# Coordinates of segments 1 to 3: a store and broadcast loads in place of TensorE products

## Chip, core and metric

One core of a Trainium2 chip runs the whole program. The metric is the device time of one execution in microseconds; the time of the kernel before is the median of three runs.

## The reference

Two layers (L0, L1) of deformable attention with an MLP, on `x` of shape 2 x 128 x 32 x 32 in float32. Per layer and batch image:

```
xn  = bn1(x);  q = gconv1x1(xn, qw)                       # 8 groups of 16 channels
off = tanh(pw @ gelu(depthwise6x6_stride4(q) + b)) * 4     # an 8x8 grid of offsets per group
n   = 2 * (grid + off) / 7 - 1                             # normalised x and y of each key
kv  = bilinear_sample(xn, n);  k, v = gconv1x1(kv, kw), gconv1x1(kv, vw)
pos = grid_q - n;  t = sign(pos) * log1p(|pos|)            # 1024 queries x 64 keys, 2 features
bias = w3 . relu(w2 . relu(w1 . t + b1) + b2) + b3         # MLP per query and key, 32 wide
x   = x + out_w @ softmax(q k / 4 + bias) v + out_b
x   = x + w2 @ gelu(w1 @ bn2(x) + b) + b                   # channel MLP 128 -> 512 -> 128
```

Bilinear sampling is written as a product with hat functions: the weight of image pixel (y, x) for a key is max(0, 1 - |cx - x|) * max(0, 1 - |cy - y|), where cx, cy are the key's pixel coordinates.

## The kernel before

The work is a chain of four segments (`SEGS` = 2 layers x 2 images), each with four units (pairs of groups) of 16 steps: 64 steps a segment, 256 in all. One step is a slice of the position-bias MLP for 128 keys: VectorE makes the hidden layer (`first_layer`, L638) into one of three `h1` buffers, TensorE adds corrections (L861) and layer 2 (L887) into two PSUM pairs, ScalarE takes each pair out with a relu (`relu2`, L484), TensorE does layer 3 (L905) of the step before into `scores`.

Every engine has its own instruction stream in an order written out by hand. `BEFORE_SLOTS` gives, for each stage that prepares the next segment, the step of the current segment behind which each engine does it; `AFTER_SLOTS` and `SOFTMAX_SLOTS` do so for attention, MLP and softmax. `plan()` collects them; within a step, softmax stages come ahead of preparing ones. Engines meet through semaphores only. In a step, ScalarE first does the second relu of the step before, then the first relu of this one, then the copy of the scores where one is due, then the planned stages. VectorE does its layer first, then the planned stages. TensorE does corrections and layer 2, then the planned stages, then layer 3.

PSUM has three pairs of banks that go round in a ring (`ring()`): each step takes two, and each planned TensorE stage one more. A pair is used again only when its last user has emptied it.

The preparation of a segment, around the change: `positions` (L670, VectorE) makes pixel coordinates `coord[:, 3]`, one key per partition, 8 columns (4 pairs, x and y). `spread` (L959, TensorE) multiplies each column, broadcast to 128 columns, by the identity, so that every partition gets all 128 x 8 coordinates in a PSUM pair. `features` (L527, ScalarE) makes sign and logarithm of the positions for the bias MLP. `spread_out` (L537, ScalarE) turns the x half into distances `hat_x` and copies the y half to `key_y`, which lies in `work`. `distances` (L544, ScalarE, four parts of two) makes |cy - y| for eight row blocks in `hat_y`. `hats` (L729, VectorE, two parts) turns distances into negated hats; the first part also does `hat_x`. `hat_products` multiplies them: four on GpSimd (L460), four on VectorE (L738). `sample` (L968, TensorE) multiplies them with the transposed image, `sample_out` (L744, VectorE) and `keys_values` (L981, L556) follow. `features_sign` (L686, VectorE) makes the features that SP stores (`store_features`, L378) and loads again spread over partitions (`load_features`, L388).

SP issues all DMAs in program order: per segment the store of features, the loads of the unit, the store of the `fy` parts, then per unit loads, and the two turns of the softmax denominators through DRAM (`invert_sums`).

Of the kernel before, what the change touches and what calls it, by code (L numbers as in the profile page):

```python
# [7 lines left out]
F32 = mybir.dt.float32  # L8
# [57 lines left out]
for _name, _n in [("ident", 128), ("gridq", W), ("gridkv", 2), ("neg_x", 1), ("neg_y", CHUNKS), ("ones", 32), ("own", 2),  # L66
# [11 lines left out]
    ("pool", "conv_products", 1): 31, ("dve", "conv_products", 0): 31, ("dve", "conv_products", 1): 32,  # L78
    ("pe", "image_t", 0): 30, ("act", "image_t_out", 0): 30, ("dve", "conv_sum", 0): 33,
    ("dve", "conv_sum", 1): 34, ("act", "conv_gelu", 0): 33, ("pe", "offset", 0): 35,  # L80
    ("act", "offset_tanh", 0): 35, ("dve", "positions", 0): 38, ("pe", "spread", 0): 37,
    ("act", "features", 0): 37, ("act", "spread_out", 0): 37, ("dve", "features_sign", 0): 40,
    ("act", "distances", 0): 39, ("act", "distances", 1): 40, ("act", "distances", 2): 41,
    ("act", "distances", 3): 42, ("dve", "hats", 0): 43, ("dve", "hats", 1): 45,
    ("pool", "hat_products", 0): 43, ("pool", "hat_products", 1): 45, ("dve", "hat_products", 0): 46,
    ("dve", "hat_products", 1): 47, ("pe", "sample", 0): 48, ("dve", "sample_out", 0): 50,
    ("pe", "keys_values", 0): 51, ("act", "keys_values_out", 0): 51,
}


# [111 lines left out]
PLACE = ring()  # L202


def build(nc, x_in, consts, weights, x_out, features_dram, fy_dram, reciprocals_dram):
    with ExitStack() as ctx:
        def sb(name, shape, dt=F32):
            return ctx.enter_context(nc.sbuf_tensor(name, shape, dt))
# [67 lines left out]
        gelu_ready = sem("gelu_ready")  # L276
        pos_ready = sem("pos_ready")
        logs_ready = sem("logs_ready")
        feat_ready = sem("feat_ready")
        feat_stored = sem("feat_stored")  # L280
        fy_ready = sem("fy_ready")
# [79 lines left out]
        def _(sp):  # L361
            def invert_sums(half):
# [12 lines left out]
                src = bass.AP(tensor=r.tensor, offset=r.offset, ap=[[HALF, G], [0, DH], [1, HALF]])  # L375
                sp.dma_start(den, src).then_inc(reciprocals_spread, 16)

            def store_features(seg):  # L378
                sp.wait_ge(feat_ready, seg + 1)
                sp.dma_start(features_dram[seg].rearrange("c u k q -> k (c u) q"), feat[:]).then_inc(feat_stored, 16)  # L380
# [49 lines left out]
            for unit in range(UNITS):  # L430
                seg, pair = unit // PAIRS, unit % PAIRS
                if pair == 0:
                    store_features(seg)
                    load_features(unit)
                    store_fy(seg)
                else:
                    load_features(unit)
                load_fy(unit)
                if pair < 2 and seg:
                    invert_sums(2 * (seg - 1) + pair)  # L440
# [37 lines left out]
        def _(act):  # L478
# [58 lines left out]
            def spread_out(seg):  # L537
# [3 lines left out]
                emptied("spread", seg, act.activation(hat_x[:], here[:, bank(0)], ACT.Abs, bias=cst("neg_x")))  # L541
                emptied("spread", seg, act.activation(key_y, here[:, bank(1)], ACT.Copy))

            def distances(n):  # L544

                wait_emptied(act, "spread", n // 4)
                for k in (2 * (n % 4), 2 * (n % 4) + 1):
                    act.activation(hat_y[:, k], key_y, ACT.Abs, bias=cst("neg_y")[:, k:k + 1]).then_inc(distances_ready, 1)

# [39 lines left out]
            def gelu_last(part):  # L589
                for c in range(MLP_PARTS):  # L590
# [3 lines left out]

            stages = {"q_out": q_out, "gelu_last": gelu_last, "image_t_out": image_t_out, "conv_gelu": conv_gelu,
                      "offset_tanh": offset_tanh, "features": features, "spread_out": spread_out,
                      "distances": distances, "attend_out": attend_out,
                      "keys_values_out": keys_values_out, "exp": exp, "widen_max": widen_max,
                      "mlp_gelu": mlp_gelu}
# [20 lines left out]
        def _(dve):  # L620
# [48 lines left out]

            def positions(seg):  # L670
                wait_emptied(dve, "offset", seg)
                if seg >= 1:
                    wait_filled(dve, "spread", seg - 1)
                    dve.wait_ge(logs_ready, 2 * seg)
                for xy in range(2):
                    ordered(dve.tensor_scalar(coord[:, 0, PAIRS * xy:PAIRS * (xy + 1)], tanh[:, xy], OFF_SCALE,
                                              cst("gridkv")[:, xy:xy + 1], ALU.mult, ALU.add))
                ordered(dve.tensor_scalar(coord[:, 1], coord[:, 0], 2.0, 1.0 / (HD - 1), ALU.mult, ALU.mult))
                ordered(dve.tensor_scalar(coord[:, 2], coord[:, 1], -1.0, None, ALU.add))
                ordered(dve.tensor_scalar(coord[:, 1], coord[:, 2], 1.0, W / 2.0, ALU.add, ALU.mult))  # L680
                ordered(dve.tensor_scalar(coord[:, 3], coord[:, 1], -0.5, None, ALU.add))
                dve.tensor_tensor(pos[:], cst("gridq").unsqueeze(1).broadcast_to([128, 2 * PAIRS, W]),
                                  coord[:, 2].unsqueeze(2).broadcast_to([128, 2 * PAIRS, W]), ALU.subtract)\
                    .then_inc(pos_ready, 1)
# [44 lines left out]
            def hats(n):  # L729

                dve.wait_ge(distances_ready, CHUNKS // 2 * (n + 1))
                if n % 2 == 0:
                    dve.tensor_scalar(hat_x[:], hat_x[:], 1.0, 1.0, ALU.min, ALU.subtract).then_inc(hat_x_ready, 1)
                    dve.wait_ge(hat_x_ready, n // 2 + 1)
                y = hat_y[:, 4 * (n % 2):4 * (n % 2) + 4]
                dve.tensor_scalar(y, y, 1.0, 1.0, ALU.min, ALU.subtract).then_inc(hats_ready, 1)  # L736
# [443 lines left out]
```

## Time and profile before

| | |
|---|---|
| median of 3 runs | 901.35 us (900.37 to 902.82) |
| profiled execution | 902.57 us, its span 900.7 us |
| TensorE busy | 812.3 us (90%) |
| VectorE busy | 714.7 us (79%) |
| ScalarE busy | 676.0 us (75%) |
| GpSimd busy | 69.1 us (8%) |
| products of `spread` (L964) | 64 instructions, 9.8 us busy |
| `spread_out` (L541, L542) | 4 each, 2.7 and 2.4 us busy |
| mean TensorE clock granted | 0.979 of full |

Busy shares are means over the whole span; a stage has its own limit, which the timelines show. In the rows, PE is TensorE, DVE VectorE, ACT ScalarE, POOL GpSimd, SP the queue that issues DMAs.

### The profile page before, as it was taken

Reading aid. Unit: us, or ns where it says so; the run is one execution under the profiler, and the core shown is the slowest. Engines: PE = TensorE matmul, PEld = TensorE weight load, DVE = VectorE, ACT = ScalarE, POOL = GpSimd, SP = SyncE. Lnnn points to the kernel's source line nnn. Section 1 sums busy time; section 2 is a strip of 40 time slices with the busy share of each in tenths; the row PEclk is TensorE's granted clock in tenths of the full one; section 3 lists DMA queues with packets and bytes.
Section 4 is the critical chain, followed back from the end, with each engine's and each line's share of the span. In section 5 each row is a group of like instructions: output and inputs, shape, how many; then the busy total and the mean of one; then the engine's idle time right before and its main releaser. Section 6 shows DMA issues by size and latency. Waiting matters only on the chain.

```text
span 900.7 us, 27769 instructions
## 1 busy us (share of the span) xinstructions
PE 812.3 (90%) x12470; PEld 232.4 (26%) x12470; DVE 714.7 (79%) x498; ACT 676.0 (75%) x775; POOL 69.1 (8%) x40
## 2 busy tenths in 40 slices
PE   2299998899999999788999999988999999999997
PEld 1122222222222222222222222222222222222224
DVE  4699798898876688989885868889888668989843
ACT  1368777978786687896877777797777677888863
POOL 2120013210000004030000000302000000000000
PEclk8589999999999999999999999999999999999999
DMA  4310101020020101002020100102002010100000
GB/s 150 80 30 25 28 9 45 7 53 4 14 54 14 50 3 50 9 3 55 3 64 15 49 4 3 50 8 53 4 4 64 14 50 2 50 27 2 2 15 24
DMA packets 23510, 26.77 MB, mean 30 GB/s; under 512 B 15328, under 2 KB 17504, under 8 KB 23392
## 3 DMA queue, kind: packets, MB, share of 16 engines
q1 hardware_dynamic: 23392, 24.99, 10.4%
q8 instruction: 99, 1.62, 0.8%
q14 instruction: 19, 0.16, 0.1%
HBM read 22.79 MB, written 2.08 MB: 28 GB/s over the span
## 4 chain that ended last, share of the span: by engine, by line
PE 42%; issue 39%; ACT 9%; DVE 5%; POOL 5%; DMA 1%; SPq 0%; ACTq 0%; POOLq 0%
PE pair L887 14%; PE scores L905 13%; ACT h L484 5%; PE pair L861 4%; DVE h L638 3%; POOL conv_prod L356 3%; PE pair L1040 2%; POOL big L464 2%; PE scores L916 2%; PE pair L995 1%; PE pair L1013 1%; PE pair L1031 1%; PE scores L1001 1%; ACT big L586 1%; PE pair L940 1%
## 5 line engine op out<-in xcount | busy, mean ns | idle before, releaser
L638 DVE TENSOR_TENSOR h<-hx,hy 128x2048 f32<-128x2048 f32 x256 | 582.1, 2302 | 76.5 <-PE pair L887 72.4
L484 ACT ACTIVATE h<-pair 128x1024 f32<-128x1024 f32 x512 | 517.6, 1024 | 146.9 <-PE pair L861 104.7
L887 PE MATMUL pair<-h,wts 32*32 32x512 f32 x8192 | 300.6, 605 | 20.5 <-DVE h L638 6.1
L905 PE MATMUL scores<-h,wts 128*32 128x512 f32 x2048 | 275.7, 607 | 0.1
L861 PE MATMUL pair<-fy,u_rows 32*128 32x512 bf16 x1024 | 102.6, 387 | 17.1 <-DMA fy<-fy_dram 17.1
L887 PEld LDWEIGHTS pair<-h,wts 32*32 32x32 f32 x8192 | 66.0, 103 | 82.2 <-ACT h L484 34.7
L861 PEld LDWEIGHTS pair<-fy,u_rows 32*128 32x128 bf16 x1024 | 26.4, 91 | 234.4 <-issue 234.4
L905 PEld LDWEIGHTS scores<-h,wts 128*32 128x32 f32 x2048 | 42.2, 108 | 158.0 <-issue 149.2
L356 POOL TENSOR_TENSOR conv_prod<-qpad,wts 128x288 f32<-128x288 f32 x16 | 34.0, 2153 | 417.7 <-ACT qpad L511 417.7
L464 POOL TENSOR_TENSOR big<-big,hat_x 128x512 f32<-128x512 f32 x16 | 32.4, 2054 | 126.6 <-DVE big L736 126.6
L995 PE MATMUL pair<-const,probs 128*128 128x128 f32 x128 | 20.6, 284 | 21.6 <-ACT h L484 20.8
L494 ACT ACTIVATE probs<-scores,wts 128x512 f32<-128x512 f32 x32 | 22.0, 688 | 23.7 <-PE scores L905 23.5
L765 DVE TENSOR_REDUCE neg_max<-pair 128x8 f32<-128x512 f32 x32 | 22.1, 690 | 20.9 <-PE pair L995 20.9
L916 PE MATMUL scores<-qpad,keys_t 128*32 128x512 f32 x256 | 33.3, 592 | 0.0
L1031 PE MATMUL pair<-work,wts 128*128 128x512 f32 x56 | 27.3, 613 | 0.5
L1040 PE MATMUL pair<-big,wts 128*128 128x512 f32 x56 | 25.9, 605 | 1.1 <-ACT big L586 1.0
L995 PEld LDWEIGHTS pair<-const,probs 128*128 128x128 f32 x128 | 13.7, 143 | 49.8 <-issue 48.1
L794 DVE SCALAR_TENSOR_TENSOR x<-pair,wts,x 128x512 f32<-128x512 f32 x7 | 5.3, 752 | 25.9 <-PE pair L1040 25.9
L578 ACT ACTIVATE probs<-scores,wts 128x512 f32<-128x512 f32 x32 | 21.9, 685 | 3.0 <-PE scores L1001 2.8
L586 ACT ACTIVATE big<-pair,wts 128x512 f32<-128x512 f32 x28 | 17.7, 684 | 8.5 <-PE pair L1031 8.4
L1001 PEld LDWEIGHTS scores<-ident_r,neg_max_wide 128*128 128x128 f32 x128 | 17.2, 190 | 24.4 <-ACT neg_max_wide L572 16.5
L1001 PE MATMUL scores<-ident_r,neg_max_wide 128*128 128x128 f32 x128 | 22.9, 302 | 0.6 <-ACT neg_max_wide L572 0.6
(101 smaller groups left out, 375.0 us busy)
## 6 DMA issues: line engine op xcount, KB each, us to landing
hx<-features_dram SPq DMA_DIRECT2D x64, 128.0 KB, 2.7
hy<-features_dram SPq DMA_DIRECT2D x64, 128.0 KB, 3.1
wts<-weights_dram SPq DMA_DIRECT2D x2, 960.0 KB, 8.4
att_den<-reciprocals_dram SPq DMA_DIRECT2D x7, 256.0 KB
x<-x_dram SPq DMA_DIRECT2D x2, 512.0 KB, 5.7
fy<-fy_dram SPq DMA_DIRECT2D x64, 6.0 KB
fy<-fy_dram SPq DMA_DIRECT2D x64, 4.0 KB
fy<-fy_dram SPq DMA_DIRECT2D x64, 2.0 KB
```

What stands on the lines that cost most here:

```text
L356: return engine.tensor_tensor(out, window, taps, ALU.mult)
L464: pool.tensor_tensor(bilinear[:, k], hat_y[:, k], hat_x[:], ALU.mult).then_inc(bilinear_ready[0], 1)
L484: emptied("z", 2 * g + j, act.activation(h2[j][g % H2_BUFS][:].rearrange("p r n -> p (r n)"), pair_of("z", 2 * g + j)[:], ACT.Relu))
L638: dve.tensor_tensor(h1[g % H1_BUFS][:].rearrange("p c (y x) -> p c y x", x=W), hx[unit % 2][:, :, t].unsqueeze(2).broadcast_to([128, CT, H ...
L861: return pe.matmul(z_of(g, r), u_rows[unit // PAIRS // B][key_rows(r)], y.unsqueeze(2).broadcast_to([32, H // 2, W]), **flags)
L887: ins = pe.matmul(z_of(g, r)[32 * c:32 * (c + 1)], w(l, "w2")[key_rows(r), key_rows(r)], h1[g % H1_BUFS][key_rows(r), c], start=r >= 2, st ...
L905: ins = pe.matmul(scores[phase % 2][32 * r:32 * (r + 1)], w(l, "w3")[:, 32 * t:32 * (t + 1)], h2[rows[0] // 2][step % H2_BUFS][:, r % 2], ...
L916: ins = pe.matmul(scores[phase % 2][k], keys_t[seg % 2][:, u, k], qpad[seg % 2][:, 1 + H // 2 * h:1 + H // 2 * (h + 1), 1:W + 1], start=Fa ...
L995: ins = pe.transpose(pair_of("scores_t", phase)[:, s], probs[:, unit % PAIRS, bank(h)][:, s], cst("ident"))
L1001: ins = pe.matmul(scores[phase % 2][:, 128 * k:128 * (k + 1)], neg_max_wide[:, 2 * k:2 * (k + 1)].rearrange("p n j -> p (n j)"), ident_r[: ...
L1031: ins = pe.matmul(pair_of("mlp_up", n)[:, bank(k)], w(half // 2 // B, "mlp_w1")[:, 128 * c:128 * (c + 1)], xn2[:, bank(half % 2)], start=T ...
L1040: ins = pe.matmul(pair_of("mlp_down", half)[:, 0:HALF], w(half // 2 // B, "mlp_w2")[:, 128 * c:128 * (c + 1)], mlp_h[:, c, bank(half % 2)] ...
```

## The change

For segments 1 to 3, the products of `spread` and the two copies of `spread_out` go. SP stores `coord[:, 3]` to DRAM, 4 bytes at a time (`store_coords`), and, behind the store of the features, loads it twice with a partition step of 0 into all 128 partitions: the x half into `hat_x`, the y half into `key_y` (`load_coords`). ScalarE then makes the distances in x in place (`hat_x_distance`, step 40). The first segment, prepared before the loop, keeps the products. The stages behind the coordinates move later: `distances` by two steps (39-42 to 41-44), `hats` and `hat_products` by two, `sample`, `sample_out` and `keys_values` by three.

```diff
-    ("act", "offset_tanh", 0): 35, ("dve", "positions", 0): 38, ("pe", "spread", 0): 37,
-    ("act", "features", 0): 37, ("act", "spread_out", 0): 37, ("dve", "features_sign", 0): 40,
-    ("act", "distances", 0): 39, ("act", "distances", 1): 40, ("act", "distances", 2): 41,
-    ("act", "distances", 3): 42, ("dve", "hats", 0): 43, ("dve", "hats", 1): 45,
-    ("pool", "hat_products", 0): 43, ("pool", "hat_products", 1): 45, ("dve", "hat_products", 0): 46,
-    ("dve", "hat_products", 1): 47, ("pe", "sample", 0): 48, ("dve", "sample_out", 0): 50,
-    ("pe", "keys_values", 0): 51, ("act", "keys_values_out", 0): 51,
+    ("act", "offset_tanh", 0): 35, ("dve", "positions", 0): 38, ("act", "features", 0): 37,
+    ("dve", "features_sign", 0): 40, ("act", "hat_x_distance", 0): 40, ("act", "distances", 0): 41,
+    ("act", "distances", 1): 42, ("act", "distances", 2): 43, ("act", "distances", 3): 44, ("dve", "hats", 0): 45,
+    ("dve", "hats", 1): 47, ("pool", "hat_products", 0): 45, ("pool", "hat_products", 1): 47,
+    ("dve", "hat_products", 0): 48, ("dve", "hat_products", 1): 49, ("pe", "sample", 0): 51, ("dve", "sample_out", 0): 53,
+    ("pe", "keys_values", 0): 54, ("act", "keys_values_out", 0): 54,
...
+            def store_coords(seg):
+
+                sp.wait_ge(pos_ready, seg + 1)
+                sp.dma_start(coords_dram[seg].rearrange("n k -> k n"), coord[:, 3], allow_slow_non_contiguous=True)\
+                    .then_inc(coords_stored, 16)
+
+            def load_coords(seg):
+                for k in range(2):
+                    sp.wait_ge(bilinear_ready[k], 4 * seg)
+                sp.wait_ge(coords_stored, 16 * seg)
+                for dst, n in ((hat_x[:], 0), (key_y, PAIRS)):
+                    c = coords_dram[seg, n]
+                    sp.dma_start(dst, bass.AP(tensor=c.tensor, offset=c.offset, ap=[[0, 128], [1, 128 * PAIRS]]))\
+                        .then_inc(coords_loaded, 16)
...
                 if pair == 0:
+                    if seg:
+                        store_coords(seg)
                     store_features(seg)
+                    if seg:
+                        load_coords(seg)
                     load_features(unit)
...
+            def hat_x_distance(seg):
+
+                act.wait_ge(coords_loaded, 32 * seg)
+                act.activation(hat_x[:], hat_x[:], ACT.Abs, bias=cst("neg_x")).then_inc(hat_x_distanced, 1)
+
             def distances(n):
 
-                wait_emptied(act, "spread", n // 4)
+                if n // 4:
+                    act.wait_ge(coords_loaded, 32 * (n // 4))
+                else:
+                    wait_emptied(act, "spread", 0)
...
             def positions(seg):
                 wait_emptied(dve, "offset", seg)
+                if seg == 1:
+                    wait_filled(dve, "spread", 0)
+                if seg >= 2:
+                    dve.wait_ge(coords_stored, 16 * (seg - 1))
                 if seg >= 1:
-                    wait_filled(dve, "spread", seg - 1)
                     dve.wait_ge(logs_ready, 2 * seg)
...
                 if n % 2 == 0:
+                    if n:
+                        dve.wait_ge(hat_x_distanced, n // 2)
                     dve.tensor_scalar(hat_x[:], hat_x[:], 1.0, 1.0, ALU.min, ALU.subtract).then_inc(hat_x_ready, 1)
```

## Rows read from the trace of the kernel before

**Rows 1.** Windows, steps 28 to 51: length, busy us (instructions) by engine, clock, DMA, GB/s.
```profile
127.20:206.20 79.00, 69.36 (x1160) 20.81 (x1156) 71.05 (x56) 65.15 (x76) 18.02 (x8) 1.00 0.13 33
...
772.90:835.90 63.00, 61.83 (x1064) 15.46 (x1060) 56.00 (x30) 51.19 (x55) 0.00 (x0) 1.00 0.09 28
```

**Rows 2.** Timeline of PE, steps 37 to 40: start, duration, instruction [idle before <-releaser].
```profile
157.88 1.17 PE L887 MATMUL pair<-h,wts 32*32 32x512 f32 x32
160.16 2.02 PE L964 MATMUL pair<-const,coord 128*128 128x128 f32 x16 [1.11 <-ACT h L484]
...
164.52 1.15 PE L887 MATMUL pair<-h,wts 32*32 32x512 f32 x32 [1.02 <-ACT work L542]
...
166.93 1.17 PE L887 MATMUL pair<-h,wts 32*32 32x512 f32 x32
...
170.21 1.17 PE L887 MATMUL pair<-h,wts 32*32 32x512 f32 x32
```

**Rows 3.** Timeline of ACT, steps 37 to 45.
```profile
163.31 0.67 ACT L541 ACTIVATE hat_x<-pair,const 128x512 f32<-128x512 f32 x1
163.88 0.59 ACT L542 ACTIVATE work<-pair 128x512 f32<-128x512 f32 x1
...
169.05 1.32 ACT L548 ACTIVATE big<-work,const 128x512 f32<-128x512 f32 x2
...
184.87 1.28 ACT L578 ACT_TABLE_LOAD   x1
186.16 0.69 ACT L578 ACTIVATE probs<-scores,wts 128x512 f32<-128x512 f32 x1
```

**Rows 4.** Timeline of PE, steps 42 to 52.
```profile
178.33 0.63 PE L995 MATMUL pair<-const,probs 128*128 128x128 f32 x4 [1.65 <-ACT h L484]
...
189.04 1.15 PE L887 MATMUL pair<-h,wts 32*32 32x512 f32 x32 [0.83 <-DVE h L638]
...
196.98 1.95 PE L976 MATMUL pair<-big,image_t 128*32 128x128 f32 x64
...
202.77 1.17 PE L887 MATMUL pair<-h,wts 32*32 32x512 f32 x32
...
206.21 1.17 PE L887 MATMUL pair<-h,wts 32*32 32x512 f32 x32
...
210.32 1.15 PE L887 MATMUL pair<-h,wts 32*32 32x512 f32 x32 [0.84 <-ACT values L564]
```

**Rows 5.** Timeline of DVE, steps 40 to 47.
```profile
163.44 0.43 DVE L690 TENSOR_TENSOR pos_sign<-pos_sign,pos_abs 128x256 f32<-128x256 f32 x1 [0.97 <-ACT pos_abs L535]
...
174.23 1.23 DVE L736 TENSOR_SCALAR big<-big 128x2048 f32<-128x2048 f32 x1
...
179.00 0.69 DVE L765 TENSOR_REDUCE neg_max<-pair 128x8 f32<-128x512 f32 x1 [1.34 <-PE pair L995]
...
182.19 3.37 DVE L638 TENSOR_TENSOR h<-hx,hy 128x2048 f32<-128x2048 f32 x1
...
186.62 2.28 DVE L638 TENSOR_TENSOR h<-hx,hy 128x2048 f32<-128x2048 f32 x1
188.82 1.28 DVE L742 TENSOR_TENSOR big<-big,hat_x 128x512 f32<-128x512 f32 x2
```

**Rows 6.** DMA view, 163 to 170 us: queue, share of 16 engines; issue, us to landing.
```profile
q1 hardware_dynamic: 1040, 0.13, 11.6%
...
features_dram<-pos_sign SPq DMA_DIRECT2D x1, 128.0 KB, 2.3
```

**Rows 7.** Source view of L399, loads of the features into partitions.
```profile
DMA to landing us min/median/max: 2.2/2.9/3.8
```

**Rows 8.** Timeline of POOL, first convolution products and first hat products inside the loop.
```profile
131.97 10.15 POOL L356 TENSOR_TENSOR conv_prod<-qpad,wts 128x288 f32<-128x288 f32 x4 [80.72 <-ACT qpad L511]
175.53 7.87 POOL L464 TENSOR_TENSOR big<-big,hat_x 128x512 f32<-128x512 f32 x4 [33.42 <-DVE big L736]
```

**Rows 9.** Source view of L759, the second hidden term: duration ns min/median/max.
```profile
L759 DVE TENSOR_SCALAR hy<-hy,wts x16: 745/748/1770, 35.2 to 814.2; 128x1024 f32<-128x1024 f32 x16
```

More of the change, by code:

```diff
@@ L202, with build @@
 PLACE = ring()
-def build(nc, x_in, consts, weights, x_out, features_dram, fy_dram, reciprocals_dram):
+def build(nc, x_in, consts, weights, x_out, coords_dram, features_dram, fy_dram, reciprocals_dram):
     with ExitStack() as ctx:
@@ L278, in build @@
         logs_ready = sem("logs_ready")
+        coords_stored = sem("coords_stored")
+        coords_loaded = sem("coords_loaded")
+        hat_x_distanced = sem("hat_x_distanced")
         feat_ready = sem("feat_ready")
@@ L596, in _ @@
                       "offset_tanh": offset_tanh, "features": features, "spread_out": spread_out,
+                      "hat_x_distance": hat_x_distance,
                       "distances": distances, "attend_out": attend_out,
@@ L1173 @@
     out = nc.dram_tensor("out_dram", (B, C, HW), F32, kind="ExternalOutput").ap()
+    coords = nc.dram_tensor("coords_dram", (SEGS, 2 * PAIRS, 2 * NKV), F32, kind="Internal").ap()
     features = nc.dram_tensor("features_dram", (SEGS, 2, PAIRS, 2 * NKV, W), F32, kind="Internal").ap()
@@ L1176 @@
     reciprocals = nc.dram_tensor("reciprocals_dram", (2 * SEGS, G, HALF), F32, kind="Internal").ap()
-    build(nc, *args, out, features, fy_parts, reciprocals)
+    build(nc, *args, out, coords, features, fy_parts, reciprocals)
     r = run_bass_kernel_spmd(nc, [arrays], core_ids=[0])
```

## The prediction

> **What bounds the kernel now.** I number the steps inside a segment from 0 to 63; step k is TensorE's (PE's) k-th pass through layer 2 (L887), and the numbers below are those of the first segment, which prepares the second; the other two repeat it within a microsecond. I first compared equal stretches of steps (28 to 51) with the view of windows [rows 1]: with preparation 79.0, 78.7 and 79.5 us, in the last segment, which prepares nothing, 63.0. Only these 16 us, three times, are touched by the change. In them VectorE (DVE) is busy for 71.05 of 79.00, PE for 69.36 and ScalarE (ACT) for 65.15, so no engine alone is the limit and the timelines must say whose turn it is.
>
> The timeline of PE around the products [rows 2]: a free step takes 164.52 to 166.93 = 2.42 us, a step with queries and keys 166.93 to 170.21 = 3.28. Step 37 takes 157.88 to 164.52 = 6.64: PE waits 1.11 for a PSUM pair, spends 2.02 on the products, and waits 1.02 more at the end, put down to ACT's L542, since step 38 needs the pair that the spread coordinates occupied. ACT's timeline [rows 3] shows why: ahead of the relu that frees the next pair it does the features, ending with the logarithm, for which DVE waits until 163.44 [rows 5], then L541 and L542 (0.67 and 0.59). From there ACT is nearly gapless to 189.6. Steps 42 and 46 show the hand-over [rows 4]: the transposes at 178.33 wait 1.65 for ACT, but step 46 at 189.04 waits 0.83 for DVE. DVE's timeline [rows 5] has its last long pause before 179.00 (1.34) and then runs without one to beyond step 48. So: ACT first, DVE from about step 45.
>
> **The change part by part.** For the coordinates: out go 16 PE instructions (2.02), a ring entry, L541 and L542 (1.26 on ACT); in come one ACT pass over 128x512 in SBUF (0.71, one of the pair at 169.05 [rows 3]), a store and two loads on SP.
>
> The transfers. Coordinates are ready at about 158.1, the features at 163.87 [rows 5], where SP stores them as before, and only then issues the two loads. The trace has no store of 4-byte pieces. The nearest row is the feature store: 1024 pieces of 128 B, 1040 packets taking 11.6% of 16 engines over 7 us = 12.5 ns each, landed after 2.3 us [rows 6]. I take 2.3; a piece would have to cost about ten times as much (64 per engine, over 100 ns) to land later than 166, which is where it starts to matter. Both ends stay in: nothing, or a late arrival (rival D). The loads, issued at some 164.4 and 165.0, land after 2.2 to 3.8 us going by other broadcast loads [rows 7], so by 168.8. SP has nothing else until step 48 lets it load the next unit, so nothing queues behind them. The Trainium skill, "DMA: Bandwidth & Descriptors", "Rules for kernel authors", says that a strided last dimension lowers to one descriptor per element; that speaks against the store and is the 1024 pieces counted here, but no run shows their price.
>
> The walk without the products. Features still end at 163.4. The two relus behind them run 163.3 to 165.25, so step 39 starts at 165.27 in place of 166.93, step 40 at 168.55 (170.21). ACT reaches the new pass at 170.7, two us after the loads; I cost that wait at nothing. Step 41 starts at 170.97. Then copy of scores (0.69) and the first pair of distances (1.32) stand ahead of the relu that frees the pair for the transposes: they start at 176.15, not 178.33, and DVE's maximum at 176.85, not 179.00 [rows 4, 5]. Lead so far: 2.15.
>
> But ACT has got later work. The distances, at steps 39 to 42 before, now stand at 41 to 44, the last pair behind the table load and exponential of step 44 (1.28 and 0.69 [rows 3]). Step 45 starts at 183.9, the exponential ends at 185.85, the distances at 187.1, two relus at 188.95: step 46 starts at 189.0 against 189.04. ACT's lead is gone; afterwards ACT has room.
>
> DVE now holds the first hats at step 45, the second at 47, its products at 48 and 49, and GpSimd's (POOL's) four products start only behind the first hats, at 183, not at 175.5. Here the price is a wait that both engines show. In the trace before, POOL's four products run 175.53 to 183.40 [rows 8], two of them under DVE's work: the layer of step 45 takes 3.37 in place of 2.28 [rows 5], the second hidden term 1.77 in place of 0.75 [rows 9]. So one product costs DVE 1.09 when DVE has no pause, and the pause before 179.00 has hidden the other two. After the change that pause lies ahead of the hats (174.5 to 176.85), so none is hidden: 4 x 1.09 = 4.36. The Trainium skill, "SBUF — State Buffer", "SBUF: two separate sides", calls the pair of ports of these engines an exclusive lock for the whole instruction. The rows of step 45 agree; the page does not say who gets it next when both wait, which rival C turns on.
>
> DVE from 176.85, start to start: maximum 0.60; hidden terms 1.40; layer of step 45 2.20 (186.62 to 188.82 [rows 5]); hats 1.60 (1.23 less the overlap, and an estimated 0.46 for a quarter of the columns); layers 46 and 47 4.40; hats 1.14; layer 48 2.20; products 1.20; layer 49 2.20; products 1.20; layers 50 to 52 6.60; maximum of step 52 0.69. Sum 25.43, with 4.36 for POOL 29.79: it ends at 206.64. Step 51 of PE needs that maximum, since the pair of the transposes comes next in the ring. It starts at 206.65 against 206.21 [rows 4]: 0.45 late. PE alone, from 189.0 with 2.42 + 3.28 + 2.42 + 2.42 + 3.44 (a step with transposes, 202.77 to 206.21 [rows 4]), would be there at 202.98.
>
> At step 51 the kernel before has its sampling behind it (at 196.98, 1.95 busy [rows 4]; about 1.75 net) and pays for keys and values, 206.21 to 210.32 less 2.42 = 1.69. Now sampling is still to come, 1.75; keys and values at step 54, without the widening of the maximum beside them on ACT, cost about 1.1, so 0.6 less. Per segment 0.45 + 1.75 - 0.6 = 1.6 us lost; three segments 4.8. From step 55 on PE alone sets the pace in both, so nothing is given back.
>
> The profiled execution took 902.57 (span 900.7 and 1.87 around it), which is 1.22 above the median of 901.35. 902.57 + 4.8 = 907.4, as a median **906.2**.
>
> **The rivals.** A is the forecast. B, the faster side: POOL's products cost DVE nothing, because they slip between its instructions. Then DVE's 202.28 is no bound, step 51 starts at 202.98, 3.23 early, less 1.75 plus 0.6: 2.1 gained per segment, 6.2 in all, median 895.1. For it: ACT and PE do lose 4.2 us of step 37, and step 42 is 2.15 earlier on any account. Against it: the rows of 3.37 and 1.77. It decides when less than 1.6 of the 4.36 is really paid.
> E: the lock costs what it did before, two products (2.2 saved against A). Then 0.6 is gained per segment: median 899.5, within what can be told from no change.
> C: POOL gets no turn while DVE is busy. POOL's first convolution products have waited so: four took 10.15 us at 131.97 [rows 8], against 7.87 for four hat products, which did get their turns. Step 51 is then early (203.0), but sampling waits until DVE pauses at 204.6 and POOL has done 4.5 us of products: 209.1, 5.0 late. 1.4 more per segment than A, median 910.4.
> D: the store of small pieces, or the loads, come after ACT at 170.7; every us beyond goes into ACT's chain and on to the transposes. A store of 12 us (against 2.3) brings the loads in at some 174.5, 4 us more per segment than A: 918.
>
> **How the numbers follow.** A 0.45, E 0.20, B 0.17, C 0.12, D 0.06. My walk can be off by 0.7 us per segment, so A's own range is 904 to 908.5. The 8 in 10 range goes from 896.5, nearly B, to 911, beyond C. What a measurement can tell from no change is 0.3%, 2.7 us. Slower: most of A, C and D, 0.57. Within: E, the near edge of A and of B, 0.22. Faster: B and a rest of E, 0.21.
>
> **What would show it.** Right, if step 38 starts less than 4 us behind step 37, step 39 leads by about 1.7, step 46 has no lead, layers and products of DVE at steps 47 and 48 show 1.1 us more, and PE waits for DVE at steps 49 to 51 (some 4 us in a segment). B shows DVE's rows at 2.28 and 0.68; C a POOL product of over 8 us and PE waiting at the sampling; D ACT idle ahead of the new pass on a DMA. I am wrong in the main step if DVE is not what PE waits for at step 51.

## The result and the profile after

The changed kernel takes 917.57 us (median of 4 runs, 913.54 to 919.09) against 901.59 in the runs beside it: ratio 1.0166, 95% interval 1.0145 to 1.0188. That is 16 us slower; the forecast was 5 us slower (906.2), its range ended at 911. Direction right, size wrong by a factor of three. The profiled execution took 919.09, its span 917.3, and the mean clock granted to TensorE fell from 0.979 to 0.963.

Windows over the same steps 28 to 51 of the three segments, columns as in [rows 1] (the last three are clock, DMA share, GB/s), and then two short ones around step 39 of the first segment:

```profile
126.40:211.60 85.20, 73.47 (x1084) 18.08 (x1080) 72.38 (x55) 65.62 (x76) 22.18 (x8) 0.92 0.14 36
348.50:433.00 84.50, 73.69 (x1089) 18.30 (x1086) 72.66 (x55) 66.10 (x77) 22.01 (x8) 0.92 0.16 37
570.00:652.20 82.20, 71.22 (x1084) 17.83 (x1080) 72.42 (x55) 66.00 (x77) 22.00 (x8) 0.94 0.16 38
...
163.00:166.40 3.40, 1.94 (x32) 0.50 (x29) 2.85 (x6) 2.21 (x3) 0.00 (x0) 1.00 0.16 25
166.40:170.00 3.60, 2.84 (x12) 0.50 (x15) 1.31 (x2) 1.94 (x2) 0.00 (x0) 0.52 0.39 78
```

The two short ones in the kernel before:

```profile
163.00:166.40 3.40, 2.38 (x48) 0.51 (x44) 1.99 (x6) 3.07 (x5) 0.00 (x0) 1.00 0.24 39
166.40:170.00 3.60, 3.60 (x60) 0.88 (x56) 3.48 (x2) 3.24 (x5) 0.00 (x0) 1.00 0.00 0
```

Against 79.0 us at a clock of 1.00 in the first stretch before, the stretches take 82 to 85 at 0.92 to 0.94: the full-speed clock (2.4 GHz) was not granted all the time. In the first short window PE has work for only 1.94 of 3.40 us (2.38 before), and behind that the granted clock is 0.52 (1.00 before), nearly the lower level of 1.2 GHz.

PE's timeline of the changed kernel, steps 38 to 51 (L922 is layer 2, L887 before; compare [rows 2, 4]):

```profile
160.95 1.15 PE L922 MATMUL pair<-h,wts 32*32 32x512 f32 x32 [0.53 <-ACT h L505]
...
164.35 0.39 PE L896 MATMUL pair<-fy,u_rows 32*128 32x512 bf16 x2 [0.92 <-issue]
165.26 1.12 PE L922 MATMUL pair<-h,wts 32*32 32x512 f32 x24 [0.52 <-issue]
167.16 2.30 PE L922 MATMUL pair<-h,wts 32*32 32x512 f32 x8 [0.78 <-issue]
169.40 1.94 PE L940 MATMUL scores<-h,wts 128*32 128x512 f32 x8
...
173.48 1.17 PE L922 MATMUL pair<-h,wts 32*32 32x512 f32 x32
...
211.57 1.15 PE L922 MATMUL pair<-h,wts 32*32 32x512 f32 x32 [1.85 <-DVE neg_max L800]
```

Step 39 takes 165.26 to 173.48 = 8.22 us; before it took 3.28. Layer 2 breaks off after 24 of 32 instructions with a gap that the trace puts to nothing ("issue"), and then everything runs at half speed: the eight products of L940 need 1.94 in place of 1.07. In the second and third segment step 39 takes 6.85 and 4.95. At step 51 PE waits 1.85 for DVE's maximum, as forecast.

The transfers, in SP's timeline of the changed kernel (start, time to issue, DMA):

```profile
157.37 0.39 SPq L383 DMA_DIRECT2D coords_dram<-coord  x1
163.87 0.38 SPq L397 DMA_DIRECT2D features_dram<-pos_sign  x1
167.66 0.34 SPq L392 DMA_DIRECT2D hat_x<-coords_dram  x1
```

The loads go when the store of the coordinates has landed, the wait that the waits of SP's queue name ahead of them: some 10.3 us after its issue. In the other segments the store and the loads stand at 379.81 and 390.13, and at 601.27 and 610.22: 10.3 and 9.0.

Steps 28 to 56, from the starts of layer 2, in us (before; after; difference): 94.20, 101.68, 7.48; 93.94, 100.47, 6.53; 94.75, 98.32, 3.57. Together 17.6, less 1.0 gained outside these steps (0.9 of it ahead of the first step 28): 16.6 in the span. They split so. Step 39 at half clock, 4.91 (its length with a fast store, below) less 3.28 = 1.63, three times: 4.9. What step 39 (and 40) takes beyond 4.91: 3.31, 2.26, 0.04 = 5.6. Steps 34 and 35, at half clock for a while: 0.87, 0.96, 0.20 = 2.0. The rest is 5.1; the forecast walk, which is all that I had, says 4.8. Half clock is granted at step 46 of each segment too (0.57 to 0.59), but it costs nothing: steps 45 to 52 take 26.9 us with it here and without it in the first segment of e4 below.

### The profile page after: what moved, and what is told of

It reads as the page before. It is cut to its first block, busy times and chain, and to the rows that moved or that the text cites. A ratio compares the mean times of both kernels' runs of the same rounds, so it can differ in the third digit from the quotient of the medians.

```text
span 917.3 us, 27682 instructions
## 1 busy us (share of the span) xinstructions
PE 825.4 (90%) x12422; PEld 229.1 (25%) x12422; DVE 720.9 (79%) x498; ACT 674.6 (74%) x772; POOL 81.7 (9%) x40
## 4 chain that ended last, share of the span: by engine, by line
PE 56%; issue 18%; ACT 12%; DVE 10%; POOL 2%; DMA 0%; SPq 0%; ACTq 0%; POOLq 0%
PE pair L922 19%; PE scores L940 17%; ACT h L505 8%; DVE h L668 6%; PE pair L896 5%; PE pair L1075 3%; PE scores L951 3%; PE pair L1030 2%; PE pair L1048 2%; PE pair L1066 2%; POOL conv_prod L358 2%; PE scores L1036 1%; DVE big L771 1%; DVE big L777 1%; ACT big L615 1%
## 5 line engine op out<-in xcount | busy, mean ns | idle before, releaser
L505 ACT ACTIVATE h<-pair 128x1024 f32<-128x1024 f32 x512 | 517.0, 1024 | 165.4 <-PE pair L896 115.7
L922 PE MATMUL pair<-h,wts 32*32 32x512 f32 x8192 | 307.9, 613 | 22.4 <-ACT h L505 7.3
L940 PE MATMUL scores<-h,wts 128*32 128x512 f32 x2048 | 281.4, 619 | 0.1
L896 PE MATMUL pair<-fy,u_rows 32*128 32x512 bf16 x1024 | 105.9, 391 | 24.6 <-DMA fy<-fy_dram 16.8
L922 PEld LDWEIGHTS pair<-h,wts 32*32 32x32 f32 x8192 | 66.8, 104 | 86.7 <-ACT h L505 38.8
L940 PEld LDWEIGHTS scores<-h,wts 128*32 128x32 f32 x2048 | 42.3, 109 | 163.4 <-issue 154.7
L485 POOL TENSOR_TENSOR big<-big,hat_x 128x512 f32<-128x512 f32 x16 | 44.9, 2837 | 160.7 <-DVE big L771 160.7
L951 PE MATMUL scores<-qpad,keys_t 128*32 128x512 f32 x256 | 36.0, 636 | 0.0
L1036 PEld LDWEIGHTS scores<-ident_r,neg_max_wide 128*128 128x128 f32 x128 | 17.2, 190 | 24.4 <-ACT neg_max_wide L601 16.5
```

The lines of the kernel that those rows point to most:

```text
L485: pool.tensor_tensor(bilinear[:, k], hat_y[:, k], hat_x[:], ALU.mult).then_inc(bilinear_ready[0], 1)
L505: emptied("z", 2 * g + j, act.activation(h2[j][g % H2_BUFS][:].rearrange("p r n -> p (r n)"), pair_of("z", 2 * g + j)[:], ACT.Relu))
L896: return pe.matmul(z_of(g, r), u_rows[unit // PAIRS // B][key_rows(r)], y.unsqueeze(2).broadcast_to([32, H // 2, W]), **flags)
L922: ins = pe.matmul(z_of(g, r)[32 * c:32 * (c + 1)], w(l, "w2")[key_rows(r), key_rows(r)], h1[g % H1_BUFS][key_rows(r), c], start=r >= 2, st ...
L940: ins = pe.matmul(scores[phase % 2][32 * r:32 * (r + 1)], w(l, "w3")[:, 32 * t:32 * (t + 1)], h2[rows[0] // 2][step % H2_BUFS][:, r % 2], ...
L951: ins = pe.matmul(scores[phase % 2][k], keys_t[seg % 2][:, u, k], qpad[seg % 2][:, 1 + H // 2 * h:1 + H // 2 * (h + 1), 1:W + 1], start=Fa ...
```

## The experiments

Theory after the result: two things were missing from the walk. (1) Without the products PE has too little to do in steps 37 to 39, and its clock falls. (2) The store of 1024 pieces of 4 bytes takes 10 us to complete and holds things up while it is open. Rivals: the later steps alone cost all; falls of the clock come anyway; any store would do the same. Ratios are to the kernel before, run beside each (901.6 us), with 95% intervals.

**e1_warm**: the clock alone. In step 37 eight products of constants, which nothing reads, stand in for the removed ones.

```diff
+            def warm(seg):
...
+                for n in range(2 * PAIRS):
+                    ins = pe.matmul(pair_of("warm", seg)[:, 128 * n:128 * (n + 1)], cst("ident"), cst("ident"), start=True, stop=True)
...
```

> The changed kernel, with eight identity products of 128 columns put back on TensorE at step 37; nothing reads them, and the coordinates still come by DMA. Clock theory (the products had filled TensorE's wait for ScalarE in steps 37 and 38; without them it idles, its clock is granted at half behind step 39, and step 39 takes 8.2, 6.9 and 5.0 us in place of 3.3): the half clock behind step 39 goes, step 39 is back at 3.3 to 4.3, some 8 to 10 us in all, 907 to 910. Store theory (the store of 4-byte pieces, some 10 us till it has landed, holds up instruction fetches and loads, and the clock falls because of that): step 39 stays long, 914 to 918. Slots theory (all of the loss comes from the later slots and the lock of VectorE and GpSimd): no change, 917.

Measured: 918.12, 1.0173 (1.0154 to 1.0191), no gain. The half clock behind step 38 was gone in all three segments, but step 39 still took 4.33, 3.28 and 5.50, and step 38 of the second 3.27, with stalls at full clock as in this row of PE's timeline (1.17 is the usual length):

```profile
165.51 2.22 PE L922 MATMUL pair<-h,wts 32*32 32x512 f32 x32
```

The loads came at 168.99, and ACT's new pass waited 1.12 for them; half clock came elsewhere, at steps 35, 42 and 51 (4.68, 5.94 and 5.77 us long). The filler does what it should at step 39, but the total is no better: the store theory had 914 to 918, the slots theory 917.

**e2_short_spread**: the clock in the kernel before. Of its 8 products of 128 columns only one is left in segments 1 to 3, so seven of the eight columns of coordinates are left out; slots, waits and ACT's copies stay.

```diff
-                for n in range(2 * PAIRS):
+                for n in range(1 if seg else 2 * PAIRS):
```

> The kernel before, with one of the eight products in segments 1 to 3 and the other seven left out; ring, ScalarE's copies and slots as before, no DMA for coordinates. Clock theory: TensorE idles 1.8 us more in step 37, its clock falls behind it in two or three segments, 2 to 3.4 us each: 905 to 911, though work has been taken out. Store theory and slots theory: nothing in this kernel can cost; step 38 waits for ScalarE's copies in any case, 900 to 902.

Measured: 905.5, 1.0037 (1.0027 to 1.0048): work taken away from PE made the kernel slower. PE's timeline, and windows around it:

```profile
159.54 0.46 PE L964 MATMUL pair<-const,coord 128*128 128x128 f32 x2 [1.11 <-ACT h L484]
...
163.91 1.64 PE L887 MATMUL pair<-h,wts 32*32 32x512 f32 x32 [2.59 <-ACT work L542]
165.48 1.94 PE L905 MATMUL scores<-h,wts 128*32 128x512 f32 x8
...
167.90 1.17 PE L887 MATMUL pair<-h,wts 32*32 32x512 f32 x32
```
```profile
157.00:164.00 7.00, 3.30 (x64) 0.94 (x70) 5.90 (x7) 6.93 (x11) 0.00 (x0) 1.00 0.01 2
164.00:168.00 4.00, 4.00 (x59) 0.57 (x71) 2.69 (x3) 1.80 (x2) 0.00 (x0) 0.57 0.20 33
```

The 1.56 us of products that went became wait for ACT's L542 (2.59 in place of 1.02 [rows 2]); then the clock is 0.57, and step 38 takes 3.99 in place of 2.41. The same happens in the third segment (steps 38 and 39); in the second a fall came at step 34, and none behind step 38. So with PE idle there the clock falls in two segments of three, without any of the rest of the change.

**e3_no_store**: the changed kernel without its store, the loads reading rows of the input; only the waits for the store go with it.

```diff
...
-                    c = coords_dram[seg, n]
+                    c = x_in[0, n]
...
```

> The changed kernel without the store of the coordinates: the two loads read rows of the input x instead, at the same place in the queue's order, so the sampling has other coordinates. Clock theory: the half clock behind step 39 stays, step 39 takes 5 to 6.7 in all three segments; only the waits for instructions in the first segment go (1 to 1.5 us): 913 to 917. Store theory: step 39 is back at 3.3, 906 to 908.

Measured: 911.89, 1.0106 (1.0082 to 1.013), between the two theories. Step 39 takes 4.83, 4.94 and 4.91: the stalls are gone, the half clock stays. The store is worth 5.7 us between the medians.

**e4_slots_only**: the kernel before with only the later steps.

```diff
-    ("act", "distances", 0): 39, ... ("dve", "hats", 0): 43, ... ("pe", "sample", 0): 48, ...
+    ("act", "distances", 0): 41, ... ("dve", "hats", 0): 45, ... ("pe", "sample", 0): 51, ...
```

> The kernel before with nothing but the later slots (distances 41 to 44, hats 45 and 47, products 48 and 49, sampling 51, keys and values 54). Clock theory and my walk for the lock: no half clock behind step 39, as the products are there; step 51 starts some 2 us later than before, 1.2 more from sampling, keys and values; 3.2 per segment, 910 to 912. Slots theory: the whole loss, 915 to 918. Store theory: 901 to 903.

Measured: 912.64, 1.011 (1.0091 to 1.013). Steps 28 to 56 take 99.77, 97.27 and 97.26. In the second that is 3.33 more than before; the first has 2.2 on top from half clock in steps 35 and 36, ahead of anything that the edit moves. Steps 45 to 52 take 26.9 in all three segments here, and 26.9 in all three of the changed kernel, although PE has half clock within them in five of these six segments and full clock in one (the first here): PE does not set the pace there.

**e5_warm_no_store**: e3 and e1 together, that is e1's products in step 37, no store, and loads from the input.

> The changed kernel with both: the eight idle products back at step 37, and no store of the coordinates (the loads read rows of x, so the sampling has other coordinates). Three-part theory (later slots with the lock, about 1.6 to 3 us a segment; the store, which holds up instructions and then the loads; half clock behind step 38): the last two are gone, what is left is my walk, 905 to 909, with step 39 at 3.3 and step 40 leading the kernel before by 1 to 1.7. Rival (the falls of the clock do not follow the idling at step 38 but come somewhere in each segment in any case): 911 to 914 as without the store alone.

Measured: 911.27, 1.011 (1.0092 to 1.0128); 905 to 909 was expected. Step 39 takes 3.28 in all three segments, but half clock came at steps 34 to 36 and 51, and the total is the rival's (911 to 914). Without those falls a segment loses some 2.2: the 1.6 of the walk and about 0.5 that the filler itself costs (steps 37 and 38 take 7.91 in place of 7.41). Against e3 the filler gained 0.6 in all.

**e6_slots_no_pool**: e4 with GpSimd's hat products cut to one column in segments 1 to 3, for the price of the lock (in the rows, the wait of VectorE and GpSimd for each other); the other columns are left out.

```diff
-                    pool.tensor_tensor(bilinear[:, k], hat_y[:, k], hat_x[:], ALU.mult).then_inc(bilinear_ready[0], 1)
+                    (pool.tensor_tensor(bilinear[:, k, 0:(1 if seg else 512)], hat_y[:, k, 0:(1 if seg else 512)], hat_x[:, 0:(1 if seg else 512)], ALU.mult)).then_inc(bilinear_ready[0], 1)
```

> The kernel before with only the later slots, and GpSimd's four hat products a segment cut from 512 columns to 1 in segments 1 to 3 (the other columns are left out). Lock theory: VectorE's layers and products of steps 46 to 50 lose their 1.1 us each, step 51 comes 3 to 4 us sooner in each segment: 901 to 905 in place of 912.6. Rival (the late sampling, keys and values and ScalarE's order are what costs): 911 to 913.

Measured: 906.34, 1.0056 (1.003 to 1.0081), with a wide spread (900.59 to 911.04): a little above the 901 to 905 expected, and far from the rival's 911 to 913. The profiled execution took 902.83. DVE's timeline from the maximum of step 44 to the layer behind that of step 52, first e6, then e4:

```profile
177.36 0.69 DVE L765 TENSOR_REDUCE neg_max<-pair 128x8 f32<-128x512 f32 x1 [2.21 <-PE pair L995]
...
187.61 1.23 DVE L736 TENSOR_SCALAR big<-big 128x2048 f32<-128x2048 f32 x1
...
202.82 2.28 DVE L638 TENSOR_TENSOR h<-hx,hy 128x2048 f32<-128x2048 f32 x1
```
```profile
180.27 0.69 DVE L765 TENSOR_REDUCE neg_max<-pair 128x8 f32<-128x512 f32 x1 [2.21 <-PE pair L995]
...
191.55 2.29 DVE L736 TENSOR_SCALAR big<-big 128x2048 f32<-128x2048 f32 x1
...
209.95 2.27 DVE L638 TENSOR_TENSOR h<-hx,hy 128x2048 f32<-128x2048 f32 x1
```

25.46 us without the products of POOL, 29.68 with them: 4.22, where the walk had 4.36.

**e7_contig_store, e8_contig_early**: another form of the store, 128 pieces of 32 bytes (a key's 8 coordinates), one load of all 512 KB into `work` ahead of the features' store, ACT reading with a step of 8 elements; e7 with the later steps, e8 with those of before.

```diff
+        spread_coord = work[:].rearrange("p (k n) -> p n k", n=2 * PAIRS)
...
-                sp.dma_start(coords_dram[seg].rearrange("n k -> k n"), coord[:, 3], allow_slow_non_contiguous=True)\
-                    .then_inc(coords_stored, 16)
+                sp.dma_start(coords_dram[seg], coord[:, 3]).then_inc(coords_stored, 16)
...
```

> The changed kernel with the store in the order of the tile, 32 bytes a partition in one piece (128 pieces in place of 1024), one load of all 4 KB into every partition ahead of the store of the features, and ScalarE reading the coordinates with a step of 8. Store part of the theory: the store lands in some 2 us, no engine waits for instructions, like the kernel without a store: 910 to 913. If it is not the pieces of 4 bytes that are slow: 916 to 919. A read with a step of 8 may cost ScalarE something; nothing expected.

> The same store and load, with the slots of the kernel before (distances 39 to 42, hats 43 and 45, products 46 and 47, sampling 48, keys and values 51) and the distances in x at step 38. Three-part theory: the slots part goes too, ScalarE saves 0.5 us and step 42 leads by 1.2, but the half clock behind step 38 stays (some 2 us where it falls): 899 to 905. Slots-only rival: 898 or less.

Measured: e7 921.34, 1.0215 (1.0195 to 1.0235); e8 910.51, 1.0094 (1.0079 to 1.0109); both lie above all that was expected. The store is fast (issued at 157.08 in e7, the load behind it at 158.50) and step 39 is at 4.9, yet e7 is the slowest of all. The reason is a cost that I had not thought of. ACT's timeline of e8:

```profile
162.92 1.24 ACT L567 ACTIVATE hat_x<-work,const 128x512 f32<-128x512 f32 x1
...
166.07 2.36 ACT L580 ACTIVATE big<-work,const 128x512 f32<-128x512 f32 x2
```

Read with a step of 8, a pass takes 1.24 in place of 0.71 and a pair 2.36 in place of 1.32 (changed kernel, below): 0.53 and four times 1.04, 4.7 us of ACT in each segment. At step 42 PE waits for ACT (2.65 us in the first segment of e7), and half clock follows there in all six segments of the two kernels. So these two do not tell what the store costs.

**e9_transposed**: the fast store without that. VectorE turns the coordinates in blocks of 32x32 and SP stores 32 pieces of 128 bytes; the rest is the changed kernel.

```diff
-                sp.dma_start(coords_dram[seg].rearrange("n k -> k n"), coord[:, 3], allow_slow_non_contiguous=True)\
-                    .then_inc(coords_stored, 16)
+                for b in range(4):
+                    rows = slice(32 * b, 32 * b + 2 * PAIRS)
+                    sp.dma_start(coords_dram[seg, :, 32 * b:32 * b + 32], coord_t[rows]).then_inc(coords_stored, 16)
...
+                    ordered(dve.tensor_scalar(coord_wide[:, 0:2 * PAIRS], coord[:, 1], -0.5, None, ALU.add))
+                    ordered(dve.transpose(coord_t[:], coord_wide[:]))
...
```

> The changed kernel with another layout of the same store and nothing else of it moved: VectorE transposes the coordinates in blocks of 32x32, so that each coordinate's 32 keys lie side by side, and the store is 32 pieces of 128 bytes in place of 1024 of 4; the loads stay two and contiguous, behind the features' store. Theory (the 10 us that the 1024 pieces take to complete cost 5.7 us: instruction fetches of 3.3 to 3.5 us and late loads): the store lands in about 2 to 3 us, no fetch over 1.8 us, step 39 takes 4.9 us in all three segments (the clock's part stays), 911 to 913 us, as without the store. Rival (any store beside the fetches does it, whatever its pieces): step 39 at 5 to 8 us and 916 to 918.

Measured: 912.62, 1.0122 (1.0109 to 1.0135), as the theory said. SP's and PE's timeline:

```profile
157.80 1.28 SPq L387 DMA_DIRECT2D coords_dram<-coord_t  x4
164.07 0.39 SPq L400 DMA_DIRECT2D features_dram<-pos_sign  x1
164.57 0.50 SPq L395 DMA_DIRECT2D hat_x<-coords_dram  x1
```
```profile
165.46 1.36 PE L930 MATMUL pair<-h,wts 32*32 32x512 f32 x32 [0.52 <-ACT h L508]
166.75 1.94 PE L948 MATMUL scores<-h,wts 128*32 128x512 f32 x8
...
170.37 1.17 PE L930 MATMUL pair<-h,wts 32*32 32x512 f32 x32
```

The loads follow the features' store at once. Layer 2 of step 39 is whole, and step 39 takes 4.91 in all three segments, still at half clock (1.94 for L948). The form of the store is worth 5.0 us between the medians.

**e10_transposed_early**: that store, loads ahead of the features' store, and the steps of before (new pass in step 38).

```diff
+    ("dve", "features_sign", 0): 40, ("act", "hat_x_distance", 0): 38,
+    ("act", "distances", 0): 39, ("act", "distances", 1): 40, ("act", "distances", 2): 41,
...
                         store_coords(seg)
+                        load_coords(seg)
                     store_features(seg)
-                    if seg:
-                        load_coords(seg)
...
```

> The store as in e9_transposed, the loads issued ahead of the features' store, and preparation in the steps of the kernel before (distances in steps 39 to 42, sampling in step 48). Theory (later steps cost 1.6 us a segment by the shared lock, the clock 1.6): step 39 at 4.9, the stretch of steps 45 to 51 back to 20 to 21 us, 28 to 56 at 94 to 96 us a segment, 902 to 907 us in all. Rival (the loads land too late for distances in step 39, and ACT loses there what the lock gives back): ACT waits for the loads over 1 us in step 38 or 39, and 908 or more.

Measured: 900.76, 0.9992 (0.9981 to 1.0003), a little better than the 902 to 907 expected. In PE's timeline the fall of the clock is still there (1.69 for L948, 4.91 for step 39):

```profile
164.95 1.15 PE L930 MATMUL pair<-h,wts 32*32 32x512 f32 x32 [0.52 <-ACT h L508]
166.03 1.69 PE L948 MATMUL scores<-h,wts 128*32 128x512 f32 x8
169.86 1.17 PE L930 MATMUL pair<-h,wts 32*32 32x512 f32 x32
```

Steps 45 to 51 take 20.51, as before. From step 37 to step 40 the kernel before takes 12.33, this one 12.32: what the removed products gave, the clock took.

**e11_transposed_early_warm**: e10 with the eight filler products of e1 in step 37, wanted as the version that keeps the gain.

```diff
+    ("act", "offset_tanh", 0): 35, ("dve", "positions", 0): 38, ("pe", "warm", 0): 37, ("act", "features", 0): 37,
...
```

> e10_transposed_early with 8 idle identity products in step 37, in place of the removed ones. Theory (the fall behind step 38 is idle TensorE, and nothing else is left of the loss): step 39 at 3.3 us, 28 to 56 at 93 to 95 us, 898 to 902 us, at or a little under the kernel before. Rival (falls of the clock come elsewhere in the stretch, whatever is filled): step 39 at 3.3, but 4.7 to 6 us in one of steps 34, 35, 42 or 51 in two or three segments, and 903 to 907.

Measured: 899.52, 0.9979 (0.997 to 0.9988): 2.1 us faster than before, the only version that is. PE's timeline and windows as above:

```profile
156.74 1.17 PE L930 MATMUL pair<-h,wts 32*32 32x512 f32 x32
158.93 2.05 PE L1014 MATMUL pair<-const 128*128 128x128 f32 x16 [1.02 <-ACT h L508]
...
162.23 1.17 PE L930 MATMUL pair<-h,wts 32*32 32x512 f32 x32
...
164.65 1.17 PE L930 MATMUL pair<-h,wts 32*32 32x512 f32 x32
...
167.93 1.17 PE L930 MATMUL pair<-h,wts 32*32 32x512 f32 x32
```
```profile
163.00:166.40 3.40, 3.40 (x68) 0.81 (x56) 3.31 (x5) 3.33 (x5) 0.00 (x0) 1.00 0.31 63
166.40:170.00 3.60, 3.60 (x56) 0.65 (x48) 2.62 (x2) 3.53 (x5) 0.00 (x0) 1.00 0.02 5
```

Steps 37 to 40 take 11.19, 1.14 less than before: PE does as many columns, but step 38 no longer waits for ACT to empty the pair with the coordinates. Three such gains are 3.4; steps 34 and 35 give 1.2 of it back at half clock in the profiled execution (1.0 in the second segment, 0.2 more than before in the third). Step 42 of the third takes 1.4 longer at half clock too, but by step 51 all but 0.1 of that is made up (30.81 from step 42, 30.67 before), so steps 28 to 56 gain 2.1 in the three segments together. So the rival, that falls come elsewhere, holds in part.

**e12_store_only**: the kernel before with the slow store added ahead of the features' store, and nothing that reads it. VectorE's positions wait for it from segment 2 on, and lose their wait for the logarithms in segment 1.

```diff
+                    if seg:
+                        store_coords(seg)
                     store_features(seg)
...
```

> The kernel before with the store of 1024 pieces of 4 bytes added behind the positions of segments 1 to 3, and nothing that reads it: the TensorE products, slots and loads are those of before. Theory (the slow store delays the fetch of instructions that falls in its 10 us): one fetch of 3 us or more in each segment and 1 to 2 us of stall on one engine behind it, where that engine sets the end; the store of the features lands later, which is hidden; 902.5 to 907 us. Rival (the store costs only by the loads that wait for it): within 0.1% of before, 900.5 to 902.5.

Measured: 901.4, 1.0014 (0.9996 to 1.0032), 12 runs; eight at 899.8 to 902.1 as the kernel before, and four above its highest of 903.61, one by little (903.67) and three at 906.4 to 907.2. In the profiled one (901.14) step 39 has its 3.28 in all three segments. That goes against the theory's 1 to 2 us in each segment, and the median is where the rival has it, that the store costs only by the loads that wait for it. But the rival does not fit the changed kernel: its gap in step 39 of the first segment ends at 167.16, and the loads are issued at 167.66. Nor is it enough that PE has its full work, since e1 gave PE as many products and still stalled. So the slow store costs some 5 us within the change (e3, e9) and nothing in most runs without it; which other part of the change it takes is not shown.

## Why the prediction was wrong in size

**The steps around the products: right.** Step 38 was to start less than 4 us behind step 37 and starts 3.10 behind; steps 37 and 38 together take 7.41, 1.65 less than before, where the walk had 1.66. That step 39 starts at 165.26, with 165.27 in the walk, owes something to luck: 0.87 lost at half clock in step 35 met 0.88 by which step 28 came earlier.

**The transfers: mis-sized, the first step that failed.** I took the landing of the nearest row, 2.3 us for 1024 pieces of 128 bytes [rows 6]; it was 10.3, 10.3 and 9.0. I had named the point from which it matters, a landing later than 166, and it was passed. Rival D gives 918, close to the result, but by another way: it had ACT idle on a DMA ahead of the new pass, and ACT's timeline of the changed kernel has no such wait there (e1, with a shorter step 39, has 1.12; for a wait marked remote the trace names no instruction that ended it):

```profile
167.55 1.94 ACT L505 ACTIVATE h<-pair 128x1024 f32<-128x1024 f32 x2 [2.34 <-remote]
173.59 2.11 ACT L505 ACTIVATE h<-pair 128x1024 f32<-128x1024 f32 x2 [4.10 <-PE pair L896]
175.59 0.71 ACT L568 ACTIVATE hat_x<-hat_x,const 128x512 f32<-128x512 f32 x1
...
178.72 1.32 ACT L577 ACTIVATE big<-work,const 128x512 f32<-128x512 f32 x2
```

The 5.0 to 5.7 us (e9, e3) were lost in steps 39 and 40, in PE's gaps and a longer half clock behind them. What exactly PE waited for in the gaps stays open. Fetches of 16 KB of instructions that normally take 1.0 took 3.30 and 3.52 us beside the open store, at 162.04 and 603.09; but the third segment lost nothing by its slow fetch, the second stalled without one, and e12 had one of 3.22 at no cost. The Trainium skill, "DMA: Bandwidth & Descriptors", "Anatomy of one DMA — SWDGE (gpsimd) path", says of another issuing path that the increment of the semaphore cannot fire until the last byte is confirmed in the target memory, which can take surprisingly long with HBM (the DRAM here) as target. The trace agrees in kind: the packets of the store are over by about 159.0, the loads behind it could go at 167.66.

**The clock: not in the sum at all, the second step that failed.** The walk has step 40 at 168.55, a lead of 1.66 on [rows 2], from rows that all stood at a granted clock of 1.00 [rows 1]. With the fast store (e9) it is at 170.37, since step 39 runs at half clock: the lead that the removed products gave was paid back at once, 1.63 a segment. e2 brings the fall about in two segments of three with nothing else changed. And over all kernels: with neither the products nor a filler in step 37, the clock falls at step 39 in all 18 segments (the changed kernel, e3, e7 to e10); with either of them it falls at steps 38 to 40 in none of 21 (the kernel before, e1, e4 to e6, e11, e12).

**ACT's lead and what is late next: right.** From step 42 to step 51 the changed kernel loses 2.58 against before, 2.60 in the walk; from 51 to 55 1.23, walk 1.15. DVE's timeline of the changed kernel:

```profile
181.77 0.69 DVE L800 TENSOR_REDUCE neg_max<-pair 128x8 f32<-128x512 f32 x1 [2.21 <-PE pair L1030]
...
187.56 5.57 DVE L668 TENSOR_TENSOR h<-hx,hy 128x2048 f32<-128x2048 f32 x2
193.05 2.29 DVE L771 TENSOR_SCALAR big<-big 128x2048 f32<-128x2048 f32 x1
195.26 3.35 DVE L668 TENSOR_TENSOR h<-hx,hy 128x2048 f32<-128x2048 f32 x1
198.53 2.37 DVE L777 TENSOR_TENSOR big<-big,hat_x 128x512 f32<-128x512 f32 x2
...
211.44 2.27 DVE L668 TENSOR_TENSOR h<-hx,hy 128x2048 f32<-128x2048 f32 x1
```

From the maximum to the layer behind the next maximum it needs 29.67 us; the walk had 29.79, of which 4.36 for POOL's lock. The four delays can be read off: 5.57 against 4.48, 2.29 against 1.23 (e6), 3.35 against 2.28, 2.37 against 1.28: 4.3 in all. Rivals B (no lock), E (half of it) and C (POOL starved) are out; POOL's four products take 12.04 in place of 7.87 [rows 8], each engine waiting in turn:

```profile
187.72 12.04 POOL L485 TENSOR_TENSOR big<-big,hat_x 128x512 f32<-128x512 f32 x4 [46.49 <-DVE big L771]
```

**The sum.** 4.8 of the walk, 4.9 of clock at step 39, 5.0 of the store (e9), 2.0 of clock at steps 34 and 35: 16.7, against 16.0 between the medians and 16.5 between the profiled executions. The 2.0 is the least settled: such falls come in some kernels and segments and not in others, in the kernel before too (0.8 at step 34 of its third segment), and no run shows what decides it. The terms come from different runs, so that they meet the total within 1 us is in part chance. The later steps, which I had costed together with the products' gain, are worth 3.14, 3.26 and 3.33 a segment by steps 28 to 56 of e9 and e10 (e10 also issues the loads earlier; 11.9 us between their medians), and 3.33 by e4, which moves nothing else: they are the largest part of the loss, and what kept this data path from breaking even.

## What to carry to other kernels

Take a removed stage's gain only after asking what TensorE does in the freed time: where the rows of before stand at full clock, work taken out can come back as half clock, as it did here. A few products of constants kept the clock up at that place, but they cost time themselves and falls came elsewhere: 1.2 us better in e11 than in e10, 0.6 in e5 than in e3, and no better in e1. Spread a small column by a store only after it is turned so that its pieces are long, and look at when the waiting DMA is issued, not at when packets end. A shift of slots is an edit of its own: price it alone, with the lock of VectorE and GpSimd at the place where the stages land.

## What was not expected of the hardware

- A store of 1024 pieces of 4 bytes to DRAM was complete 9.0 to 10.3 us after its issue, one of 1024 pieces of 128 bytes 2.3 [rows 6]; while it was open, the features' store landed after 4.5 to 4.7 in place of 2.3 and fetches of instructions took up to 3.8 (e1) in place of 1.0. The Trainium skill, "VectorE: DVE Perf Modes", "The three transpose paths", warns of transposing by the strides of a plain DMA, and e9 agrees in direction: with a turn in 32x32 blocks on VectorE, which the section lists as one way, the kernel is 5.0 us faster.
- Work taken out of TensorE cost clock: where its products had gone from step 37, the granted clock of step 39 fell in all 18 segments, to 0.52 in the window above, from 1.00 before. With filler it stayed at 1.00 there, and fell in other places in eight of the nine segments of e1, e5 and e11.
- ACT reading float32 from SBUF with a step of 8 elements: 1.24 us for 128x512, against 0.71 contiguous.
- When DVE and POOL both want the lock, they take turns product by product, 1.06 to 1.09 us each time, in all four delays of the rows above; in the convolution products of [rows 8] POOL got no such turns (10.15 us for its four, the longest 7.83 and the shortest 0.81).
